# Attention scores on the two halves of TensorE's array, and one ring of eight banks

## The chip, the core and the metric

The kernel runs on one core of a Trainium2 chip. Its time is device microseconds; lower is better. TensorE (PE in the profile) multiplies and writes to PSUM, which has eight banks of 512 float elements a partition. VectorE (DVE) and ScalarE (ACT) read the banks, GpSimd (POOL) works in SBUF alone, SyncE (SP) issues the transfers.

## What is computed

Four layers over x, 4 sequences of 256 rows of 512 (8 tiles of 128 rows). Each layer normalises x, computes a gate from it (an FFN of the layer's own kind, then silu), and attention, and adds gate times attention to x. The attention, cut to what matters here:

```
q = x_n Wq -> 32 heads of 16;  k, v = x_n Wk, x_n Wv -> 8 heads (layers 0, 2, 3) or 32 (layer 1)
q, k = rope(q), rope(k)                                  # not in layer 1
s = q k^T / 4;  s = where(key <= query, s, -large)       # no mask in layer 1
out = softmax(s) v ;  x += gate * (out Wo)
```

Results are float32. Products of float32 precision are made of parts: `fp32r` operands that hold a high and a low part of each number.

## The kernel before, in words

**Units and groups.** Attention works on 8 units a layer; unit u is half of the heads (16) of sequence u // 2. A unit has 4 groups g of 4 heads, numbered through as gi = 4u + g. `project` makes q, k and v of 128 rows (tau 0 or 1), in three products in the layers with shared keys.

**Stacks.** `stack_high` (ScalarE) and `stack_low` (GpSimd) lay each head's 16 numbers out as 64: high, low, high part, then a place for the row maximum and zeros (keys: high, high, low, then a one and zeros), so that one product over 64 rows gives the precise score. `turn_stacks` turns them with TensorE, 128 columns at a time: two query heads lie under each other on 128 partitions. For keys the stack has four places, (k, 0, 0, k): turned, it gives one operand with the head's keys in the upper half and zeros in the lower, and one the other way round. ScalarE copies the turned queries to `qT` (`take_stacks`), VectorE the keys to `kT` (`take_key_stacks`).

**Scores, twice.** `scores_rows` (key "S", lines 685 and 691) makes scores with queries on the partitions, for two heads in one product of 2 x 128 or 2 x 256 columns because of the zeros, and adds the causal mask by another product (identity times mask). `row_max` (VectorE, L1370) takes the maximum. It runs LEAD = 5 groups ahead. `turn_max`, `take_max` and two transfers put the maxima into `qT` as the row that meets the one. `scores_cols` (key "ST", L719) makes the scores again with keys on the partitions, less the maximum; `exponentials` (ScalarE, L1038) empties them into `probs`; `cut_future` (GpSimd, L1572) clears the future. `weigh_values` (key "PV", L739) multiplies by the values: four heads in four column quarters of the array. `take_pv` (ScalarE) copies that out, `turn_context` (L750) turns it, `context` (VectorE, L1394, L1397) divides it. After every second unit `turn_rows` and `project_out` (L760, L780) finish a sequence, and `residual` adds it.

**Banks.** `Banks.claim` counts the uses of each bank, and TensorE waits until the earlier user is emptied. Row scores rotate over banks 0 and 1, column scores over 2 and 3, everything else (`misc_bank`) over 4 to 7. Each score bank holds one pair of heads and is emptied by itself.

**Order.** Every engine works through an order written out by hand, in `attention`. On TensorE one group is: `project` (g = 0: u+2, tau 1; g = 3: u+3, tau 0), `turn_max` (g = 3), column scores 0, stacks of one tau (g = 0: u+1, half 1; g = 2: u+2, half 0), row scores 0 of gi+5, values of gi-1, column scores 1, the stacks of the other tau, row scores 1, context of gi-2. In the last unit the next layer's normalised rows are turned too, through banks 0 and 1. The FFNs lie between the attentions.

## Time and profile before

| | |
|---|---|
| median of 3 runs | 1435.74 us (1433.23 to 1436.2) |
| profiled execution | span 1432.5 us, mean granted clock 0.970 |
| TensorE busy | 1328.4 us (93%) |
| VectorE, ScalarE, GpSimd busy | 884.6, 670.5, 389.4 us |

The span runs from the first to the last instruction; the median is 3.2 us above it. Matmuls are pipelined, so one lasts longer than the distance to the next start; distances between starts add up to time, durations don't. A row's "idle before" names what the engine waited for.

### The profile page before, as it was taken

What the parts mean: (1) busy time and instruction counts of PE and PEld (TensorE: products, weight loads), DVE (VectorE), ACT (ScalarE), POOL (GpSimd) and SP (SyncE); (2) the same over time, 40 slices, a digit from 0 to 9 for tenths busy, and PEclk for the clock granted to TensorE, in tenths of its full rate; (3) what the DMA queues carried; (4) which work ended last, traced back from release to release, by engine and by line L of the source; (5) the groups of instructions that cost most, each with busy time, mean ns of one, the idle gap of its engine ahead of it and who ended that gap; (6) DMA issues with size and microseconds to landing.
All of it is one profiled execution on the core that took longest, in us unless ns stands there. A gap on an engine that the chain in (4) does not pass through costs nothing.

```text
span 1432.5 us, 22066 instructions
## 1 busy us (share of the span) xinstructions
PE 1328.4 (93%) x8364; PEld 998.8 (70%) x8364; DVE 884.6 (62%) x1661; ACT 670.5 (47%) x1420; POOL 389.4 (27%) x470
## 2 busy tenths in 40 slices
PE   4999899997798999998899999989999879899997
PEld 3888777775465666665688888877777557677775
DVE  7733577777506655567455566467777645777873
ACT  3433365655133654556223333236565447365653
POOL 1000333323011100000433443323343346333331
PEclk9999999999799999999899999999999889999998
DMA  6000000002000000002222232100000300000001
GB/s 261 1 1 0 1 3 2 2 2 97 30 0 1 2 1 2 2 2 92 95 89 88 92 107 89 45 1 2 2 3 2 128 30 1 1 2 2 3 1 60
DMA packets 11610, 48.18 MB, mean 34 GB/s; under 512 B 2793, under 2 KB 3694, under 8 KB 10226
## 3 DMA queue, kind: packets, MB, share of 16 engines
q1 hardware_dynamic: 11506, 46.76, 9.3%
q8 instruction: 69, 1.13, 0.3%
q14 instruction: 35, 0.29, 0.1%
HBM read 44.13 MB, written 2.10 MB: 32 GB/s over the span
## 4 chain that ended last, share of the span: by engine, by line
PE 84%; DVE 10%; ACT 3%; issue 2%; DMA 1%; POOL 0%; SPq 0%; DVEq 0%; ACTq 0%
PE bank L487 18%; PE bank L647 13%; PE bank L518 9%; PE bank L719 7%; PE bank L780 7%; PE bank L685 7%; PE bank L739 7%; PE bank L665 6%; PE bank L691 3%; DVE negmaxs L1370 2%; PE bank L750 2%; DVE negmaxw L1370 2%; PE bank L588 1%; DVE stats L1127 1%; PE bank L760 1%
## 5 line engine op out<-in xcount | busy, mean ns | idle before, releaser
L1572 POOL TENSOR_SCALAR_AFFINE_SELECT probss<-probss 128x512 f32<-128x512 f32 x192 | 134.2, 700 | 334.0 <-ACT probss L1038 334.0
L1370 DVE TENSOR_REDUCE negmaxs<-bank 128x2 f32<-128x512 f32 (+1 forms) x384 | 193.7, 551 | 36.8 <-PE bank L691 35.0
L1038 ACT ACTIVATE probss<-bank 128x256 f32<-128x256 f32 (+1 forms) x384 | 167.9, 492 | 41.9 <-PE bank L719 41.4
L685 PE MATMUL bank<-kTs,qTs 128*128 128x512 f32 (+1 forms) x384 | 135.3, 411 | 5.2 <-DVE kTs L1378 2.8
L1518 POOL TENSOR_TENSOR W_lo<-W_lo_whole,W_hi 128x1536 fp32r<-128x1536 f32 x28 | 98.1, 3504 | 138.4 <-ACT W_hi L889 138.4
L719 PE MATMUL bank<-qTs,kTs 128*128 128x256 f32 (+1 forms) x384 | 117.3, 383 | 4.6 <-ACT probss L1038 3.9
L691 PE MATMUL bank<-mask,identb 128*128 128x256 bf16 x384 | 105.0, 283 | 0.0
L889 ACT ACTIVATE W_hi<-W_lo_whole 128x1536 fp32r<-128x1536 f32 x28 | 41.7, 1488 | 134.7 <-DVE W_lo_whole L1253 134.7
L1378 DVE CAST kTs<-bank 128x512 fp32r<-128x512 f32 x96 | 65.6, 689 | 50.9 <-PE bank L665 50.9
L1274 DVE TENSOR_TENSOR h_lo<-h_lo_whole,h_hi 128x512 fp32r<-128x512 f32 x50 | 73.3, 1465 | 34.9 <-ACT h_hi L911 34.9
L1378 DVE CAST kTw<-bank 128x512 fp32r<-128x512 f32 x64 | 40.9, 685 | 82.3 <-PE bank L665 82.3
L1370 DVE TENSOR_REDUCE negmaxw<-bank 128x2 f32<-128x512 f32 x128 | 81.6, 685 | 14.0 <-PE bank L685 13.6
L487 PE MATMUL bank<-xT_hi,W_hi 128*128 128x512 f32 x224 | 89.2, 398 | 0.0
L487 PE MATMUL bank<-xT_lo,W_hi 128*128 128x512 f32 x224 | 88.6, 396 | 0.0
L685 PEld LDWEIGHTS bank<-kTs,qTs 128*128 128x128 f32 x384 | 74.5, 194 | 20.0 <-DVE negmaxs L1370 11.5
L487 PE MATMUL bank<-xT_hi,W_lo 128*128 128x512 f32 x224 | 88.4, 395 | 0.0
L647 PE MATMUL bank<-Wqkv,xT_whole 128*128 128x512 f32 (+1 forms) x256 | 87.0, 495 | 0.8 <-ACT gate L922 0.8
L987 ACT ACTIVATE qks<-bank 128x320 f32<-128x320 f32 x48 | 21.1, 439 | 141.7 <-PE bank L647 141.6
L739 PE MATMUL bank<-probss,Vs 128*32 128x256 f32 (+1 forms) x1536 | 82.7, 333 | 4.0 <-issue 3.5
L911 ACT ACTIVATE h_hi<-h_lo_whole 128x512 fp32r<-128x512 f32 x72 | 45.4, 630 | 72.3 <-DVE h_lo_whole L1265 46.4
L1038 ACT ACTIVATE probsw<-bank 128x512 f32<-128x512 f32 x128 | 69.6, 599 | 16.6 <-PE bank L719 14.2
L719 PEld LDWEIGHTS bank<-qTs,kTs 128*128 128x128 f32 x384 | 60.4, 191 | 23.4 <-issue 12.7
(219 smaller groups left out, 3162.2 us busy)
## 6 DMA issues: line engine op xcount, KB each, us to landing
W_lo_whole<-in_w SPq DMA_DIRECT2D x28, 768.0 KB, 4.2
Wqkv_whole<-in_Wqkv SPq DMA_DIRECT2D x3, 1536.0 KB, 10.6
Wo_lo_whole<-in_Wo SPq DMA_DIRECT2D x4, 1024.0 KB, 6.2
Wqkv<-in_Wqkv SPq DMA_DIRECT2D x1, 3072.0 KB, 10.6
Wdown_whole<-in_Wd SPq DMA_DIRECT2D x1, 2816.0 KB, 15.2
x<-in_x SPq DMA_DIRECT2D x4, 512.0 KB, 5.9
out<-x SPq DMA_DIRECT2D x8, 256.0 KB, 2.2
V_lo_whole<-in_V SPq DMA_DIRECT2D x1, 1408.0 KB
```

Of the source, the lines that this page charges most:

```text
L487: ins = mm(ps[:], lh, rh, start=(c == 0), stop=(c == len(terms) - 1))
L518: ins = mm(B.tensor(key)[:], lh, rh, start=(j == 0 and c == 0), stop=(j == C - 1 and c == len(terms) - 1))
L647: ins = mm(ps[:, 0:width], lh, rh, start=(c == 0), stop=(c == len(terms) - 1))
L685: ins = mm(ps[:, 0:2 * nk].rearrange("p (h k) -> p h k", h=2), A[l].qT[u % 2][:, 2 * g + pl, qb * P:(qb + 1) * P], A[l].kT[u % 2][:, slot: ...
L691: ins = mm(dst, identb[:], mask[:].rearrange("p (h k) -> p h k", h=2), start=False, stop=True)
L719: ins = mm(ps[:, pairs[0] * nq:pairs[1] * nq].rearrange("p (h q) -> p h q", h=n), A[l].kT[u % 2][:, key_slot(l, g, 2 * g + pairs[0], par), ...
L739: ins = mm(ps[32 * i:32 * i + 32, q0:SEQ], A[l].Vflat[u % 4][:, (kb * A[l].vh + kv) * CELL:(kb * A[l].vh + kv) * CELL + 32], A[l].probs[gi ...
L780: ins = mm(ps[:], lh, rh, start=(c == 0), stop=(c == len(terms) - 1))
L1038: nc.scalar.activation(A[l].probs[gi % 2][:, kb, par:4:2, q0:SEQ], B.tensor(key)[:, 0:2 * nq].rearrange("p (h q) -> p h q", h=2), ACT.Exp, ...
L1370: v.tensor_reduce(A[l].negmax[u % 2][:, qb, 2 * g + pl:2 * g + pl + 9:8], B.tensor(key)[:, 0:2 * nk].rearrange("p (h k) -> p h k", h=2), A ...
L1378: v.tensor_copy(A[l].kT[u % 2][:, 4 * w:4 * w + 4, tau * P:(tau + 1) * P], B.tensor(key)[:].rearrange("p (a t) -> p a t", a=4)).then_inc(B ...
L1572: gp.affine_select(out=blk, in_=blk, compare_op=ALU.is_ge, fill=0.0, base=0, pattern=[[0, 4], [1, P]], channel_multiplier=-1).then_inc(cau ...
```

## The change

Score products use 64 rows: the heads of a pair lie in the two halves of the array, each product with its own half of `qT` and `kT`, and the two write to two neighbouring banks. The key stacks have no zero places and, where keys are shared, none twice, so a unit's turned keys are a fourth (shared) or half (layer 1) as wide. The heads are permuted on the host so that the two heads of a pair use different keys. The causal mask becomes products of 64 rows too: two for each half, each over 64 key columns of both heads.

A piece of scores, "S" or "ST" of one group and one block, now fills two banks and is emptied by one instruction of VectorE or ScalarE. All eight banks belong to one ring: pieces take banks 0-1, 2-3, 4-5, 6-7 in each group, then the ring is set to bank 0 and the values, the context and whatever follows take the next banks; `claim` waits for every earlier holder of the banks that it takes. TensorE's order within a group becomes: stacks of both taus at once (g = 0, 2), `project` and `turn_max`, then rows 0, columns 0, rows 1, columns 1, then values, context and the rest. ScalarE does both exponentials, then `stack_high`, then `take_pv`.

```diff
-    def claim(self, key, bank):
-        self.where[key] = (bank, self.uses[bank])
+    def claim(self, key, bank, n=1):
+        earlier = [self.emptied(k) for k in dict.fromkeys(self.holder[bank:bank + n]) if k is not None]
+        self.where[key] = (bank, self.uses[bank], n)
         self.uses[bank] += 1
+        self.holder[bank:bank + n] = [key] * n
+        return self.tensor(key), earlier
...
-            def misc_bank():
-                misc[0] += 1
-                return 4 + misc[0] % 4
+            def next_bank(n=1):
+                if n == 2:
+                    ring[0] += ring[0] % 2
+                bank = ring[0] % 8
+                ring[0] += n
+                return bank
...
-            def turn_stacks(l, u, tau, half):
+            def turn_stacks(l, u, half):
+                for tau in range(2):
+                    i = 2 * u + tau
                     pe.wait_ge(*pads.at(l, PADS[l]))
                     pe.wait_ge(*stack_hi.at(l, HI * (i + 1)))
                     pe.wait_ge(*stack_lo.at(l, 2 * (i + 1)))
+                    key = ("qT", l, u, tau, half)
+                    ps = claim(key, next_bank())
...
+                n = A[l].kn // 2
+                key = ("kT", l, u, half)
+                if GQA[l]:
+                    ps = claim(key, next_bank())[:, 0:2 * P].rearrange("p (t q) -> p t q", t=2)
+                else:
+                    ps = claim(key, next_bank(2), 2)
+                for tau in range(2):
+                    for p in range(n):
+                        ins = nc.tensor.transpose(ps[:, tau, p * P:(p + 1) * P].bitcast(F32R),
+                                                  A[l].kstack[tau][:, n * half + p, :, :].rearrange("p h s -> p (h s)"),
+                                                  ident_r[:])
...
+                key = ("S", l, u, g, qb)
+                ps = claim(key, bank, 2)
                 for pl in range(2):
...
-                    ins = mm(ps[:, 0:2 * nk].rearrange("p (h k) -> p h k", h=2),
-                             A[l].qT[u % 2][:, 2 * g + pl, qb * P:(qb + 1) * P],
-                             A[l].kT[u % 2][:, slot:slot + 2, 0:nk], start=True, stop=not CAUSAL[l])
+                    for par in range(2):
+                        r = slice(64 * par, 64 * par + 64)
+                        ins = mm(ps[:, par, pl * nk:(pl + 1) * nk], A[l].qT[u % 2][r, 2 * g + pl, qb * P:(qb + 1) * P],
+                                 A[l].kT[u % 2][r, key_slot(l, g, pl), 0:nk], start=(pl == 0),
+                                 stop=(pl == 1 and not CAUSAL[l]))
+                if CAUSAL[l]:
+                    for j in range(2):
+                        for par in range(2):
+                            r = slice(64 * par, 64 * par + 64)
+                            k0 = nk - P + 64 * j
+                            dst = ps[:, par, 0:2 * nk].rearrange("p (h k) -> p h k", h=2)[:, :, k0:k0 + 64]
+                            ins = mm(dst, cut_rows[r, j, :], cut_keys[r, j, :, :], start=False, stop=(j == 1))
+                ins.then_inc(B.fills(key), 1)
...
+                key = ("ST", l, u, g, kb)
+                ps = claim(key, bank, 2)
+                for pairs in ((0, 2),) if GQA[l] else ((0, 1), (1, 2)):
+                    n = pairs[1] - pairs[0]
+                    for par in range(2):
+                        r = slice(64 * par, 64 * par + 64)
+                        ins = mm(ps[:, par, pairs[0] * nq:pairs[1] * nq].rearrange("p (h q) -> p h q", h=n),
+                                 A[l].kT[u % 2][r, key_slot(l, g, pairs[0]), kb * P:(kb + 1) * P],
+                                 A[l].qT[u % 2][r, 2 * g + pairs[0]:2 * g + pairs[1], q0:SEQ], start=True, stop=True)
...
+                    if g == 0 and u + 1 < UNITS:
+                        turn_stacks(l, u + 1, 1)
+                    if g == 2 and u + 2 < UNITS:
+                        turn_stacks(l, u + 2, 0)
...
+                    for part in range(2):
+                        if ahead:
+                            scores_rows(l, gi + LEAD, part, 4 * part)
+                        scores_cols(l, u, g, part, 4 * part + 2)
+                    ring[0] = 0
                     if gi >= 1:
                         weigh_values(l, gi - 1)
                     if gi >= 2:
                         turn_context(l, gi - 2)
...
-                        transposes(l + 1, (2 * g - 2, 2 * g - 1), banks=(0, 1))
+                        transposes(l + 1, (2 * g - 2, 2 * g - 1))
...
                     exponentials(l, u, g, 0)
-                    if g == 0 and u + 1 < UNITS:
-                        take_stacks(l, u + 1, 0, 1)
-                    if g == 2 and u + 2 < UNITS:
-                        take_stacks(l, u + 2, 0, 0)
+                    exponentials(l, u, g, 1)
+                    if g < 2 and u + 2 < UNITS:
+                        stack_high(l, u + 2, g)
                     if gi >= 1:
                         take_pv(l, gi - 1)
...
+                key = ("S", l, u, g, qb)
+                dve.wait_ge(*B.filled(key))
+                v.tensor_reduce(A[l].negmax[u % 2][:, qb, :].rearrange("p (b h) -> p b h", b=2)[:, :, 2 * g:2 * g + 2],
+                                B.tensor(key)[:, :, 0:2 * nk].rearrange("p b (h k) -> p b h k", h=2),
+                                AX.X, ALU.max, negate=True).then_inc(B.empties(key), 1)
```

VectorE keeps its order: `row_max` of the first block, `rope` (g = 0 and 3), `row_max` of the second block, `context`.

## Rows read from the trace of the kernel before

**Rows 1.** The page: the chain that ended last, by engine

```profile
PE 84%; DVE 10%; ACT 3%; issue 2%; DMA 1%; POOL 0%; SPq 0%; DVEq 0%; ACTq 0%
```

**Rows 2.** Stretches (us; busy us of each engine, instructions; granted clock)

```profile
204.29:224.27 19.98, 19.94 (x179) 15.49 (x179) 15.50 (x38) 12.97 (x34) 7.83 (x13) 1.00 0.01 2
224.27:250.75 26.48, 26.44 (x212) 20.86 (x211) 19.97 (x46) 14.07 (x36) 8.78 (x13) 1.00 0.01 2
501.39:566.37 64.98, 64.61 (x429) 42.77 (x429) 37.04 (x71) 33.02 (x70) 5.72 (x8) 1.00 0.01 2
338.00:362.00 24.00, 12.93 (x122) 7.78 (x114) 20.92 (x60) 13.48 (x32) 8.46 (x11) 0.95 0.21 89
```

**Rows 3.** Timeline of TensorE, layer 0, 211.3 to 215: start, us, instruction

```profile
211.32 0.86 PE L739 MATMUL bank<-probss,Vs 128*32 128x256 f32 x16
212.11 0.38 PE L685 MATMUL bank<-kTs,qTs 128*128 128x256 f32 x1
...
212.62 0.48 PE L719 MATMUL bank<-qTs,kTs 128*128 128x256 f32 x2
213.14 0.49 PE L685 MATMUL bank<-kTs,qTs 128*128 128x512 f32 x1
...
213.95 0.38 PE L750 MATMUL bank<-ident,pvs 128*128 128x128 f32 x2
214.09 0.70 PE L719 MATMUL bank<-qTs,kTs 128*128 128x512 f32 x2
214.63 0.46 PE L665 MATMUL bank<-ident_r,qstacks 128*128 128x128 f32 x4
214.93 0.25 PE L665 MATMUL bank<-ident_r,kstacks 128*128 128x128 f32 x1
```

**Rows 4.** The chain in time, layers 0 and 1: one `project` each

```profile
218.85 2.12 PE bank L647 x12
...
472.74 5.19 PE bank L647 x16
```

**Rows 5.** Groups of VectorE, 204.29 to 250.75: busy us, mean ns, idle before

```profile
L1370 DVE TENSOR_REDUCE negmaxs<-bank 128x2 f32<-128x512 f32 x18 | 11.6, 684 | 0.8 <-PE bank L691 0.8
L1370 DVE TENSOR_REDUCE negmaxs<-bank 128x2 f32<-128x256 f32 x16 | 6.0, 419 | 0.8 <-PE bank L691 0.6
L1378 DVE CAST kTs<-bank 128x512 fp32r<-128x512 f32 x8 | 5.5, 689 | 4.9 <-PE bank L665 4.9
L1397 DVE TENSOR_TENSOR ctxs<-bank,recips 128x128 f32<-128x128 f32 x9 | 2.6, 291 | 0.3
...
L1394 DVE RECIPROCAL recips<-bank 128x8 f32<-128x8 f32 x9 | 1.8, 198 | 0.0
```

**Rows 6.** Timeline of VectorE: the first and last of rope's four products

```profile
208.81 0.48 DVE L1354 TENSOR_TENSOR rope_coss<-qks,cos 128x320 f32<-128x320 f32 x1
...
209.79 0.49 DVE L1361 TENSOR_TENSOR rope_coss<-rope_coss,rope_sins 128x320 f32<-128x320 f32 x1
```

**Rows 7.** Groups of ScalarE, 204.29 to 250.75

```profile
L1038 ACT ACTIVATE probss<-bank 128x512 f32<-128x512 f32 x16 | 8.7, 602 | 0.0
L1038 ACT ACTIVATE probss<-bank 128x256 f32<-128x256 f32 x16 | 5.3, 381 | 0.9 <-PE bank L719 0.7 <-issue 0.2
...
L1045 ACT ACTIVATE pvs<-bank 128x256 f32<-128x256 f32 x8 | 3.1, 388 | 2.9 <-PE bank L739 2.9
L1015 ACT ACTIVATE qstacks<-rope_coss 128x512 fp32r<-128x512 f32 x4 | 2.6, 638 | 0.0
L1021 ACT ACTIVATE kstacks<-rope_coss 128x128 fp32r<-128x128 f32 x8 | 2.1, 315 | 0.0
```

**Rows 8.** Groups of GpSimd, 204.29 to 250.75

```profile
L1556 POOL TENSOR_TENSOR qstacks<-rope_coss,qstacks 128x256 fp32r<-128x256 f32 x4 | 2.9, 734 | 2.0 <-ACT kstacks L1021 2.0
L1563 POOL TENSOR_TENSOR kstacks<-rope_coss,kstacks 128x128 fp32r<-128x128 f32 x4 | 1.9, 463 | 0.0
```

**Rows 9.** Timeline of TensorE at the start of layer 0's attention

```profile
167.80 0.75 PE L665 MATMUL bank<-ident_r,kstacks 128*128 128x128 f32 x4 [4.87 <-DVE kTs L1378]
```

More of the change, by code:

```diff
@@ L446, in transposes @@
                     key = ("xT", l, t)
-                    ps, again = B.claim(key, misc_bank() if banks is None else banks[t % 2])
-                    if again:
-                        pe.wait_ge(*B.before(key))
+                    ps = claim(key, next_bank() if banks is None else banks[t % len(banks)])
                     pe.wait_ge(*xn_ready.at(l, t + 1))
@@ L470, in gate_up @@
                     key = (("gate", "up")[which], l, n, j)
-                    ps, again = B.claim(key, 2 * (e % 2) + which)
-                    if again:
-                        pe.wait_ge(*B.before(key))
+                    ps = claim(key, 2 * (e % 2) + which)
                     terms = []
@@ L525, in out_tile @@
                 key = ("out", l, t)
-                ps, again = B.claim(key, bank)
-                pe.wait_ge(*B.before(key))
+                ps = claim(key, bank)
                 for c, (lh, rh) in enumerate(terms):
@@ L534, in weight_sum @@
                 key = ("wsum", m)
-                ps, again = B.claim(key, (0, 1, 4)[m])
-                if again:
-                    pe.wait_ge(*B.before(key))
+                ps = claim(key, (0, 1, 4)[m])
                 pe.wait_ge(*abs_summed.at(0, m + 1))
@@ L542, in low_rank_in @@
                 key = ("low", n)
-                ps, again = B.claim(key, n)
-                pe.wait_ge(*B.before(key))
+                ps = claim(key, n)
                 pe.wait_ge(*B.emptied(("xT", 3, 4 * n + 3)))
@@ L568, in ffn @@
                             key = ("group", c, which)
[L569 to L570 removed]
+                            ps = claim(key, (2 * c + which) % 4)
                             mm(ps[:], onehot[:, c * P:(c + 1) * P], src[:], start=True, stop=True).then_inc(B.fills(key), 1)
                         if c == 1:
[L573 removed]
+                            transposes(l, LATE_TILES, banks=(6, 7))
                     for t0 in (0, 4):
@@ L634, in project @@
                                        [(("qkv", l, u, tau), 0, 512), (("v", l, u, tau), 512, 256)]):
-                    ps, again = B.claim(key, misc_bank() if bank is None else bank)
-                    pe.wait_ge(*B.before(key))
+                    ps = claim(key, next_bank() if bank is None else bank)
                     terms = []
@@ L726, in weigh_values @@
                 key = ("PV", l, gi)
-                ps, again = B.claim(key, misc_bank())
-                pe.wait_ge(*B.before(key))
+                ps = claim(key, next_bank())
                 if CAUSAL[l]:
@@ L745, in turn_context @@
                 key = ("ctx", l, gi)
-                ps, again = B.claim(key, misc_bank())
-                pe.wait_ge(*B.before(key))
+                ps = claim(key, next_bank())
                 pe.wait_ge(*B.emptied(("PV", l, gi)))
@@ L755, in turn_rows @@
                     key = ("ctxT", l, b, tau)
-                    ps, again = B.claim(key, misc_bank())
-                    pe.wait_ge(*B.before(key))
+                    ps = claim(key, next_bank())
                     pe.wait_ge(*B.emptied(("ctx", l, 8 * b + 7)))
@@ L767, in project_out @@
                     key = ("O", l, b, tau)
-                    ps, again = B.claim(key, misc_bank())
-                    pe.wait_ge(*B.before(key))
+                    ps = claim(key, next_bank())
                     pe.wait_ge(*B.emptied(("ctxT", l, b, tau)))
@@ L788, in attention @@
                 for half in range(2):
-                    for tau in range(2):
-                        turn_stacks(l, 0, tau, half)
+                    turn_stacks(l, 0, half)
                 project(l, 2, 0)
```

314 lines of the change are left out of this document (129 added, 185 removed).

## The prediction

> **What bounds the kernel now.** The chain that ended last comes first: TensorE is on it for 84% of the span [rows 1]. The busy times by stretch say where: in layer 0's attention a unit of odd number takes 19.98 us with TensorE busy for 19.94, a unit of even number (it also turns and projects the context of a sequence) 26.48 us with 26.44, and two units of layer 1 take 64.98 us with 64.61 [rows 2]. The same rows say how near the others are: in the odd unit VectorE 15.50, ScalarE 12.97, GpSimd 7.83. So in a steady unit nothing but TensorE's work sets the time, because today no copy out of a bank is waited for: scores have banks 0 to 3, everything else turns through banks 4 to 7. The change takes work off TensorE and also takes that separation away. I therefore read both: the instructions removed, and then one unit step by step with the new waits. All my times are of the profiled execution, span 1432.5 us; the median of the runs, 1435.7, is 3.2 above it, and I add that at the end.
>
> **TensorE's score work.** One causal group today, by the starts in the timeline [rows 3]: row scores of the first query block (call them R0) from 212.11 to 212.62, 0.51 us; of the second block (R1) 213.14 to 213.95, 0.81; column scores of all queries (C0) 214.09 to 214.63, 0.54; of the late ones (C1) 212.62 to 213.14, 0.52. In sum 2.38 us. Around them: values (PV) 0.79, turning the context 0.14, four stack transposes 0.30, that is 0.075 us each.
> After the change every score matmul works on 64 rows and streams half the columns, with twice as many masks of half the width. Nothing in this trace splits the array by rows. Bounds: projection matmuls stream 384 columns in 2.12/12 = 0.177 us, 0.46 ns a column [rows 4]. Below, both halves stream at once and weights load for nothing: R0 0.24, R1 0.35, C0 0.24, C1 0.12, in sum 0.95. Above, nothing overlaps, and where matmuls are short each costs what a transpose with 128 new weight columns costs, 0.075: R0 8 x 0.075 = 0.60, R1 0.71, C0 0.47, C1 0.24, in sum 2.02. The nearest row is PV, whose matmuls use quarters of the array by columns: its 16 entries take 0.79 us, while plain fp32 entries of the whole array take 5.19/6144 columns = 0.84 ns a column [rows 4], so eight of 256 columns and eight of 128 would be 2.6 us. Quarters do run side by side, 3.3 times as fast. I take overlap for the streams but one weight load after another at 0.075: R0 0.55 (eight loads, bf16 ones a little cheaper), R1 0.60, C0 0.28, C1 0.18, in sum 1.61, 0.77 less than now.
> Of 32 stack transposes per causal unit 12 go (the zero slots and the doubled keys): 0.9 us; in layer 1 16 of 48: 1.2. Alone, this is 4 x 0.77 + 0.9 = 4.0 us off TensorE in a unit of 19.98.
>
> **What the others pay.** One reduce over two banks replaces two. The rows give 684 ns for 512 elements and 419 for 256 [rows 5], so 1.035 ns an element: 1024 elements 1.21 us (M1), and 512 elements 0.68 (M0). For the exponentials 602 and 381 [rows 7]: 1.04 us (E0) and 0.60 (E1). Only fixed parts go. The key copy falls from four of 689 ns to two of 256 elements, near 0.42 each; a second key copy on ScalarE, 0.31, goes from each stack [rows 5, 7]. These are real savings, but on engines that have slack.
>
> **What is late next: the banks.** After a group's four score pieces the ring is set to bank 0. So PV takes bank 0 and the context bank 1, both just held by R0; the next group's R0 takes banks 0 and 1 again, and `claim` waits until ScalarE has copied PV out and VectorE has finished `context`. In VectorE's order `context` stands behind both reduces and, for g = 0 and 3, behind `rope` between them: from 208.81 to 210.28 (the end of its last product), 1.47 us [rows 6]. In ScalarE's order the PV copy (0.39) stands behind both exponentials and, for g = 0 and 1, behind `stack_high` (0.64 and 0.31, which overlap a little: 0.80 for the two, an estimate) [rows 7]. And `turn_stacks` for u+2 now needs both halves at once, the second of which GpSimd ends only 1.20 us (0.73 + 0.46 [rows 8]) after `stack_high` in g = 1. Before, these were behind TensorE's back.
> I walk an odd causal unit from R0 to R0, with 0.27 us from the last matmul's start to the first use (the pair of context transposes lasts 0.38 against 0.14 to the next start [rows 3], so 0.24 and a little) and 0.06 where a wait ends. Group 1 to group 2: R0 0.55, C0 0.28, 0.25, E0 1.04, E1 0.58, stack_high 0.80, GpSimd 1.20, second query transposes 0.32, keys 0.16, waits 0.06: 5.24. Group 2 to 3: the query copy and C0's wait for it 0.75, C0 0.28, R1 0.60, 0.27, M1 1.21, 0.06, turn_max 0.14, project 2.11: 5.42. Group 3 to 0: R0 0.55, 0.27, M0 0.68, rope 1.47, M1 1.21, 0.06 (the keys' bank was R1's), keys 0.16, project 2.11: 6.51. Group 0 to 1: R0 0.55, 0.27, 0.68, 1.47, 1.21, context 0.20 + 0.29 [rows 5] with gaps 0.52, 0.06: 4.76. Sum 21.93 against 19.98: **+1.95**, although TensorE now has work for only 16 us of it.
> In an even unit the turning and projecting of the context, 26.48 - 19.98 = 6.5 us of TensorE, fills the waits of groups 2 and 3. Group 1 to 2 stays 5.24; group 2 to 3 ends with the turned rows (0.8 of the 6.5) in place of a wait, 5.81; group 3 to 0 is TensorE's own work, R0 to context 2.55 with two small waits, 5.7 of projecting, 0.7 of stacks, 2.11: 11.06; group 0 to 1 stays 4.76. Sum 26.87, **+0.39**.
> Layer 1 the same way, with M and E 1.21 and 1.04 throughout, no rope, R0 and R1 0.40, C0 and C1 0.32, `project` 5.19, key copies of 1.21 before R1: 30.0 for an odd unit and 38.4 for an even one against 64.98 for the pair: +1.4 and +2.0 by the split at the project pieces.
>
> **Starts and ends of the layers.** At a layer's start TensorE stands 4.87 us because four banks are not enough while VectorE does rope [rows 9]; with eight in the ring, and row scores that need only half 0's keys, the first reduce comes about 5 us sooner. I give each causal layer -5, layer 1 -6 (its 16 key copies become four larger ones). In the last unit (24.00 us, VectorE busy 20.92 [rows 2]) the next layer's transposes now take banks 2 and 3, which the next C0 needs: 0.8 us twice, +1.6 in three layers. Units 5 and 6, with less projecting and rope, come out 1.1 shorter together.
>
> **The sum.** Causal layers: 3 x 1.95 + 2 x 0.39 = +6.6, -1.1, -5, +1.6: +2.1, twice, and +0.5 for the last layer. Layer 1: 3 x 1.4 + 2 x 2.0 = +8.2, about -1.0 in units 5 and 6, -6, +1.6: +2.8. Total +7.5: span 1440, time **1443.5 us**. With the matmul bounds in the same walk: below, an odd unit is 1.57 shorter and an even one 1.67 (22 us over the three causal layers, 5 more in layer 1): 1416. Above, 0.7 and 1.06 longer: 1463.
>
> The Trainium skill bears on two steps. TensorEngine Tiling (Array Packing), section PSUM Bottleneck, says that tiling speeds TensorE up but not the emptying of PSUM, which may then be the limit; the trace agrees so far as VectorE has 15.5 us of work in 20. TensorE: Matmul & The Clock Gate, Part 3, says that matmuls in different row groups run concurrently; by it alone the sum would go to the lower bound, 1416. The Tiling page's Key Properties also say that a change of tiling mode drains the array, which speaks for the upper bound; no row separates such a drain.
>
> **The rivals.** (a) Slightly faster, by one mechanism: the two halves load and stream wholly at once, so the R and C pieces on the chain shrink to the lower bound. 1416, and everything between there and 1433. For it: PV's 3.3. It decides once R0 is under about 0.40 and R1 under 0.45.
> (b) The change does what it says and TensorE stays the bound: the new bank waits end before TensorE gets there. Then 4.0 us go from each causal unit (7 x 4.0 x 3 = 84), about 5 from each of layer 1's (35), and 20 at the starts: near 1300. Against it: the chain through VectorE in group 0 alone is 4.76 us, where TensorE has some 2.5 us of work.
> (c) The halves don't overlap: 1463 and somewhat more.
> (d) TensorE, idle for a quarter of each unit, is granted 1.2 instead of 2.4 GHz in the steady units: projections, PV and scores double, some 8 us a unit: 1600 and more. Against it: the last unit of layer 0 has TensorE busy for 12.93 of 24.00 us and a mean grant of 0.95 [rows 2].
> The change of the masks and the permuted heads cost nothing: host layout, and two casts more or less in layer 0's FFN behind a busy TensorE.
>
> **How the numbers follow.** My forecast, the waits eat the gain (1436 to 1455): 0.42. (a) 0.25, (b) 0.11, (c) 0.17, (d) 0.05. Within 0.2%, 2.9 us, which is about what a measurement of this kernel can tell from none, lies the seam between (a) and the forecast: 0.12, of which 0.10 is from the forecast and 0.02 from (a). Faster 0.34, slower 0.54. The likeliest case's own range is 1430 to 1460; for 8 in 10 I leave out (b)'s far end and (d): 1385 to 1480.
>
> **What would show it.** TensorE's busy share in a steady odd unit falls to about 0.75 to 0.8, with gaps before R0 ended by VectorE's `context` or ScalarE's PV copy, of 1 to 2 us in groups 0 and 1; an odd causal unit lasts 21 to 23 us; the row scores' group of eight starts about 70 ns apart; the start stall of 4.87 us shrinks. Wrong would be: gaps absent and units of 16 to 18 us (b), or starts 35 ns apart (a) or 120 ns apart (c).

## The result and the profile after

The changed kernel takes 1486.39 us (median of 4 runs, 1482.7 to 1487.8) against 1435.97 for the kernel before (1433.2 to 1440.7): ratio 1.0348, 95% interval 1.0324 to 1.0373, slower by 3.5%. The forecast, 1443.5 with a range of 1385 to 1480, had the sign and not the size; the measured time lies above the range. The profiled execution took 1486.46 us with a span of 1484.7, 52.2 more than before.

From the page of the changed kernel: the engines' shares of the chain that ended last, and the rows by slice of TensorE's busy time and granted clock.

```profile
PE   4999888887796888887799999988888679888887
...
PEclk7999889987697899999899999999898889999889
...
PE 70%; DVE 15%; ACT 6%; issue 5%; POOL 3%; DMA 1%; DVEq 0%; ACTq 0%; SPq 0%
```

TensorE's share of the chain fell from 84% [rows 1] to 70%; VectorE, ScalarE, GpSimd and "issue" took it over. The stretches that answer to [rows 2], in the same columns (length; busy TensorE, weight load, VectorE, ScalarE, GpSimd; granted clock), are two odd causal units (layer 2), an even one, and the same two units of layer 1 as before:

```profile
1002.24:1025.64 23.40, 19.38 (x198) 14.89 (x197) 13.16 (x26) 11.94 (x24) 7.31 (x13) 0.88 0.01 2
1025.64:1046.87 21.23, 17.84 (x200) 13.54 (x198) 13.37 (x28) 11.72 (x25) 7.18 (x12) 0.97 0.01 2
1046.87:1075.88 29.01, 25.85 (x232) 20.51 (x230) 17.91 (x34) 13.74 (x27) 7.34 (x12) 0.86 0.01 2
580.79:652.49 71.70, 60.13 (x428) 37.44 (x428) 30.95 (x43) 31.95 (x52) 5.66 (x8) 0.93 0.01 1
```

(The first of them is unit 0; the second, unit 1, is the plain odd unit.) TensorE's work in the odd unit is 17.84 us instead of 19.94, but the unit is longer. The clock column has something that [rows 2] hadn't: 0.97, 0.88, 0.86 and 0.93 in steady units, where before it was 1.00. One steady stretch cut at the changes of the grant, layer 2:

```profile
1013.00:1023.48 10.48, 8.19 (x92) 6.36 (x94) 7.79 (x17) 5.93 (x12) 3.72 (x6) 1.00 0.01 2
1023.48:1026.89 3.41, 3.41 (x36) 2.45 (x36) 1.92 (x2) 2.07 (x4) 0.97 (x2) 0.50 0.00 0
1026.89:1047.37 20.48, 17.09 (x202) 13.27 (x198) 12.85 (x27) 10.97 (x23) 6.21 (x11) 1.00 0.01 2
1047.37:1054.20 6.83, 5.83 (x56) 4.30 (x52) 3.33 (x6) 4.38 (x9) 2.81 (x6) 0.50 0.00 1
```

The grant drops to 0.50, that is to 1.2 GHz, for 3.41 and 6.83 us at a time. What goes before the second drop is to be seen in TensorE's timeline (start, us; in brackets idle time and what ended it), the counterpart of [rows 3]:

```profile
1043.11 0.44 PE L747 MATMUL bank<-ident,pvs 128*128 128x128 f32 x2
1045.52 0.44 PE L686 MATMUL bank<-kTs,qTs 64*128 64x128 f32 x4 [1.97 <-DVE ctxs L1374]
1045.78 0.31 PE L695 MATMUL bank<-cut_keys,cut_rows 64*128 64x128 bf16 x4
1045.88 0.50 PE L718 MATMUL bank<-qTs,kTs 64*128 64x512 f32 x2
1046.19 0.42 PE L686 MATMUL bank<-kTs,qTs 64*128 64x256 f32 x4
1046.43 0.31 PE L695 MATMUL bank<-cut_keys,cut_rows 64*128 64x128 bf16 x4
1046.52 0.39 PE L718 MATMUL bank<-qTs,kTs 64*128 64x256 f32 x2
1046.87 1.07 PE L737 MATMUL bank<-probss,Vs 128*32 128x256 f32 x16
...
1048.22 0.82 PE L655 MATMUL bank<-ident_r,qstacks 128*128 128x128 f32 x4
1050.04 0.72 PE L655 MATMUL bank<-ident_r,qstacks 128*128 128x128 f32 x4 [1.00 <-POOL kstacks L1530]
```

and in VectorE's over the same time:

```profile
1041.39 0.69 DVE L1343 TENSOR_REDUCE negmaxs<-bank 128x4 f32<-128x512 f32 x1 [2.25 <-PE bank L695]
1042.00 0.48 DVE L1329 TENSOR_TENSOR rope_coss<-qks,cos 128x320 f32<-128x320 f32 x1
...
1042.99 0.82 DVE L1336 TENSOR_TENSOR rope_coss<-rope_coss,rope_sins 128x320 f32<-128x320 f32 x1
1043.72 1.21 DVE L1343 TENSOR_REDUCE negmaxs<-bank 128x4 f32<-128x1024 f32 x1
1044.86 0.19 DVE L1371 RECIPROCAL recips<-bank 128x8 f32<-128x8 f32 x1
1045.08 0.29 DVE L1374 TENSOR_TENSOR ctxs<-bank,recips 128x128 f32<-128x128 f32 x1
```

R0 of group 1 stands 1.97 us, because its bank holds the context of group 0 and VectorE makes first maximum, rope, second maximum and context in that order, 3.98 us from 1041.39 to 1045.37. One group later the second query transposes stand 1.00 us for GpSimd's low rows, and the clock has dropped in between, at 1047.37: the matmuls after it start further apart (PV, which it catches halfway, lasts 1.07 instead of 0.86).

Whole layers, from the first start of PV(0) to that of PV(31), two rows of each timeline; in brackets what the prediction's terms add up to:

| | before | changed | difference | predicted |
|---|---|---|---|---|
| layer 0 | 162.14 | 180.34 | +18.2 | +7.1 |
| layer 1 | 211.67 | 234.47 | +22.8 | +8.8 |
| layer 2 | 160.69 | 178.89 | +18.2 | +7.1 |
| layer 3 | 156.72 | 167.93 | +11.2 | +5.5 |
| all else (starts, ends, FFNs) | | | -18.2 | -21 |

The starts did nearly what they should; the steady units did not, nor the last unit.

### The profile page after: what moved, and what is told of

The parts are those of the page before. It is cut to its first block, busy times and chain, and to the rows that moved or that the text cites. A ratio compares the mean times of both kernels' runs of the same rounds, so it can differ in the third digit from the quotient of the medians.

```text
span 1484.7 us, 22636 instructions
## 1 busy us (share of the span) xinstructions
PE 1271.3 (86%) x8844; PEld 951.8 (64%) x8844; DVE 809.6 (55%) x1309; ACT 643.4 (43%) x1100; POOL 368.6 (25%) x462
## 4 chain that ended last, share of the span: by engine, by line
PE 70%; DVE 15%; ACT 6%; issue 5%; POOL 3%; DMA 1%; DVEq 0%; ACTq 0%; SPq 0%
PE bank L490 17%; PE bank L642 12%; PE bank L520 9%; PE bank L775 7%; PE bank L737 5%; PE bank L686 4%; DVE negmaxs L1343 4%; PE bank L718 3%; PE bank L747 2%; PE bank L655 2%; DVE negmaxw L1343 2%; PE bank L667 1%; POOL probss L1539 1%; PE bank L584 1%; PE bank L695 1%
## 5 line engine op out<-in xcount | busy, mean ns | idle before, releaser
L1343 DVE TENSOR_REDUCE negmaxs<-bank 128x4 f32<-128x512 f32 x192 | 180.8, 955 | 106.9 <-PE bank L695 105.0
L1019 ACT ACTIVATE probss<-bank 128x1024 f32<-128x1024 f32 x192 | 146.8, 809 | 116.3 <-PE bank L718 115.8
L686 PE MATMUL bank<-kTs,qTs 64*128 64x128 f32 (+1 forms) x768 | 93.9, 323 | 47.2 <-DVE ctxs L1374 35.9
L686 PEld LDWEIGHTS bank<-kTs,qTs 64*128 64x128 f32 x768 | 75.9, 210 | 73.4 <-issue 45.7
L1343 DVE TENSOR_REDUCE negmaxw<-bank 128x4 f32<-128x1024 f32 x64 | 74.9, 1218 | 67.5 <-PE bank L686 67.5
L718 PE MATMUL bank<-qTs,kTs 64*128 64x256 f32 (+1 forms) x384 | 92.4, 470 | 20.4 <-DVE xT_lo L1127 7.5
L1008 ACT ACTIVATE qTs<-bank 128x512 fp32r<-128x512 f32 x96 | 54.0, 600 | 86.6 <-PE bank L655 85.3
L1019 ACT ACTIVATE probsw<-bank 128x1024 f32<-128x1024 f32 x64 | 62.8, 1023 | 38.8 <-PE bank L718 38.7
L642 PE MATMUL bank<-Wqkv_hi,xT_hi 128*128 128x384 f32 x192 | 69.7, 363 | 0.0
L655 PE MATMUL bank<-ident_r,qstacks 128*128 128x128 f32 x384 | 49.8, 273 | 22.7 <-POOL kstacks L1530 15.5
## 6 DMA issues: line engine op xcount, KB each, us to landing
Wqkv<-in_Wqkv SPq DMA_DIRECT2D x1, 3072.0 KB, 11.2
```

Of the source, the lines that this page charges most:

```text
L642: ins = mm(ps[:, 0:width], lh, rh, start=(c == 0), stop=(c == len(terms) - 1))
L655: ins = nc.tensor.transpose(ps[:, p * P:(p + 1) * P].bitcast(F32R), A[l].qstack[tau][:, 8 * half + 2 * p:8 * half + 2 * p + 2, :] .rearran ...
L686: ins = mm(ps[:, par, pl * nk:(pl + 1) * nk], A[l].qT[u % 2][r, 2 * g + pl, qb * P:(qb + 1) * P], A[l].kT[u % 2][r, key_slot(l, g, pl), 0: ...
L718: ins = mm(ps[:, par, pairs[0] * nq:pairs[1] * nq].rearrange("p (h q) -> p h q", h=n), A[l].kT[u % 2][r, key_slot(l, g, pairs[0]), kb * P: ...
L1019: nc.scalar.activation(A[l].probs[gi % 2][:, kb, :, q0:SEQ].rearrange("p (b h) q -> p b h q", b=2), B.tensor(key)[:, :, 0:2 * nq].rearrang ...
L1343: v.tensor_reduce(A[l].negmax[u % 2][:, qb, :].rearrange("p (b h) -> p b h", b=2)[:, :, 2 * g:2 * g + 2], B.tensor(key)[:, :, 0:2 * nk].re ...
```

## The experiments

All edits are of the changed kernel (1486.4 us). Ratios are to the kernel before. The share of the span at 1.2 GHz is worked out as 2 x (1 - mean clock), since there are only two levels: for the changed kernel (0.908) 18.4% or 273 us, before (0.970) 86 us.

**1. Orders: `e1_pv_copy_first`, `e2_rope_last`.** Theory 1: waits for the common banks, and the clock that falls with them, set the time. Theory 2: the 64-row matmuls themselves cost.

```diff
                     exponentials(l, u, g, 1)
+                    if gi >= 1:
+                        take_pv(l, gi - 1)          # e1
                     if g < 2 and u + 2 < UNITS:
                         stack_high(l, u + 2, g)
-                    if gi >= 1:
-                        take_pv(l, gi - 1)
```
```diff
-                    rope(l, ...)                    # e2: g = 0 and 3
                     if ahead:
                         row_max(l, gi + LEAD, 1)
                     if gi >= 2:
                         context(l, gi - 2)
+                    rope(l, ...)
```

> The changed kernel, except that ScalarE copies the weighted values out of their bank before it stacks the high rows (0.8 us in groups 0 and 1), not after. Changed kernel: 1486.4 us. Theory 1 (TensorE waits for banks of the common ring, and the idle time also brings the 1.2 GHz grants): in groups 0 and 1 the row scores may start up to 0.8 us earlier, but the stacks come later by 0.4 and most waits of the trace end with VectorE's context, so 3 to 15 us less, 1471 to 1483. Theory 2 (the matmuls of 64 rows cost TensorE more than the ones of 128 did, waits are not the matter): no change, 1483 to 1490.

> The changed kernel, except that VectorE's rope products of groups 0 and 3 (1.47 us) stand behind the second maximum and the context instead of between the two maxima. Theory 1: the row scores and the context's bank come free 1.47 us earlier in two groups of four, 2 x 21 units x up to 1.5 us = up to 60 us; the rope parts come later, which takes some back: 1440 to 1470. Theory 2: no change, 1483 to 1490.

Measured: 1519.2 (1.0584, 1.0560 to 1.0607), 33 us slower than the changed kernel, and 1458.0 (1.0167, 1.0148 to 1.0186), 28 us faster. Rope last fits theory 1. The copy's move went the other way than I said. The transposes of the query stacks, as the page groups them, say why; first the changed kernel, then e1 (busy, mean ns, then idle before and what ended most of it):

```profile
L655 PE MATMUL bank<-ident_r,qstacks 128*128 128x128 f32 x384 | 49.8, 273 | 22.7 <-POOL kstacks L1530 15.5
```

```profile
L655 PE MATMUL bank<-ident_r,qstacks 128*128 128x128 f32 x384 | 52.3, 283 | 35.1 <-POOL kstacks L1530 28.6
```

The waits for GpSimd's rows nearly double, from 15.5 to 28.6 us, while R0's 35.9 us for the context stay. What I counted as a slack of 0.4 us on the stacks was on the path, and the clock went down too (0.890, 334 us at 1.2 GHz). Theory 2 is out as the whole cause: the same matmuls in another order differ by 61 us.

**2. The old separation of banks: `e3_split_rings`, `e4_split_and_order`.**

```diff
-                bank = ring[0] % 8
+                bank = 4 + ring[0] % 4
...
-                            scores_rows(l, gi + LEAD, part, 4 * part)
-                        scores_cols(l, u, g, part, 4 * part + 2)
-                    ring[0] = 0
+                            scores_rows(l, gi + LEAD, part, 0)
+                        scores_cols(l, u, g, part, 2)
```

This is e3; the row pieces ahead of a layer's first group and the next layer's transposes go to banks 0 and 1 with it. e4 adds TensorE's and ScalarE's old order.

> The changed kernel's instructions in the changed order, but row scores always in banks 0 and 1, column scores in banks 2 and 3, all else turns through banks 4 to 7, as before the change. The waits for context and for the copy of the weighted values go. In their place the second row scores wait in the same group for the first maximum (0.68 or 1.21 us after the first row scores, with only 0.28 us of column scores between). Theory 1: a different set of waits of about the same length, 1450 to 1490. Theory 2: no change, 1483 to 1490. By itself this run tells little; it is the step to the next one.

> As the run with split banks, and TensorE's order is that of the kernel before: first column scores, first row scores, weighted values, second column scores, second row scores; ScalarE copies the weighted values between its two exponentials. All matmuls of 64 rows, the merged copies out of two banks and the smaller stacks stay. Theory 1: each wait has 0.8 us or more of TensorE work beside it, an odd causal unit takes 17.5 to 19.5 us instead of 21.2 to 23.4, the 1.2 GHz stretches become few: 1375 to 1430, faster than the changed kernel by 4% or more. Theory 2: the matmuls cost what they cost, 1470 or more.

Measured: 1566.9 (1.0925, 1.0887 to 1.0963) and 1559.2 (1.0864, 1.0816 to 1.0911). My 1375 to 1430 for e4 was a bad miss, and e3 lies far above its 1450 to 1490. Both were granted only 0.89. Rows of e4's timeline with idle time, one odd unit and a little:

```profile
1079.28 0.44 PE L642 MATMUL bank<-Wqkv_hi,xT_hi 128*128 128x384 f32 x1 [1.85 <-DVE ctxs L1375]
...
1087.98 0.44 PE L686 MATMUL bank<-kTs,qTs 64*128 64x128 f32 x4 [1.78 <-DVE negmaxs L1344]
...
1092.44 0.51 PE L655 MATMUL bank<-ident_r,qstacks 128*128 128x128 f32 x4 [1.76 <-POOL kstacks L1531]
```

Its odd units have three waits of 1.8 us in place of one of 2 and one of 1 to 1.6. One is the row scores': a piece now fills two banks, so two banks for row scores hold one piece and not two, and R0 waits for the maximum of the R1 ahead of it, a whole reduce of 1.2 us. Separate rings were free while each bank was emptied alone; emptying two at once takes the double buffering that they lived from. The other two, a projection behind the context and the stacks behind GpSimd, are not of this kind, and no run has separate rings with banks emptied singly, so how much of the 73 us above the changed kernel is the lost double buffering is not shown. The orders and rings of before alone don't give the time of before.

**3. Is the clock a cause? `e9_filler` and its control `e17_filler_elsewhere`.** If idle time brings the 1.2 GHz stretches, then useless work inside the waits must make the kernel faster.

```diff
+            def fill(ps, n):
+                for _ in range(n):
+                    nc.tensor.transpose(ps[:, 0:P].bitcast(F32R), ident_r[:], ident_r[:])
...
+                                fill(B.ps[:, 2, :], 16)    # e9: group 1, causal layers
                             scores_rows(l, gi + LEAD, part, 4 * part)
...
+                        fill(ps, 12)                       # e9: turn_stacks, half 0, tau 1
                     pe.wait_ge(*pads.at(l, PADS[l]))
...
+                            fill(B.ps[:, 2, :], 28)        # e17 instead: group 3, behind project
```

The first bank filled is one that the next column scores overwrite, and TensorE waits first until it is empty. In `turn_stacks` of e9 the claim of the bank moves ahead of the waits for the stacks, so that there is a bank to fill; nothing is issued in between. e9 adds 552 transposes in all, e17 504.

> The changed kernel with extra TensorE work that nobody reads: 16 transposes of the identity into the next column bank before the row scores of group 1 (where the trace has a wait of 1.97 us in each steady causal unit), and 12 before the second query transposes of group 2 (wait 0.3 to 1.6 us), in the three causal layers. Order, waits and all other work are unchanged; the extra transposes cost about 75 ns each where nothing is waited for. Theory A (the idle time of TensorE brings the stretches at 1.2 GHz, and these are a good part of the loss): the waits are filled, most 3.4 us stretches at 0.5 in steady causal units vanish, odd units settle at 21.2 us instead of 21.2 to 23.4: 1445 to 1475. Theory B (the lost time is the bank waits alone; the granted clock falls for another reason, such as the 64-row matmuls): the stretches stay, and time is equal or up to 25 us longer: 1484 to 1512.

> A control for the extra transposes: the changed kernel with the same kind of transposes, 28 together behind the projection of group 3, where TensorE waits for nothing, instead of 16 and 12 inside the two waits. Theory A (what helped was that TensorE was not idle in the waits): the waits of 2.0 and 1.6 us stay and the stretches at 0.5 with them, and the transposes cost 28 x 75 ns = 2.1 us and more in each of 18 units: 1515 to 1540. Theory B (more TensorE work anywhere raises the grant, or the other edit of that kernel helped): 1465 to 1500.

Measured: e9 1463.8 (1.0201, 1.0182 to 1.0220), 22.6 us **faster with more work**; e17 1533.6 (1.0688, 1.0668 to 1.0707), 47 us slower. Stretches of e9: units 1 and 2 of layer 2, and nearly all of its units 0 to 6 in one piece.

```profile
1014.94:1036.42 21.48, 19.63 (x227) 15.83 (x226) 13.48 (x28) 11.85 (x25) 7.18 (x12) 1.00 0.01 2
1036.42:1063.47 27.05, 25.57 (x261) 21.02 (x259) 17.77 (x34) 13.06 (x27) 7.36 (x12) 1.00 0.01 2
995.63:1149.23 153.60, 139.51 (x1530) 110.88 (x1529) 97.67 (x192) 79.38 (x154) 45.86 (x77) 1.00 0.08 32
```

The same stretch of layer 2 in the changed kernel, and in e17:

```profile
996.17:1139.53 143.36, 122.83 (x1204) 93.93 (x1203) 86.12 (x163) 74.54 (x144) 43.41 (x72) 0.88 0.01 2
```

```profile
1001.00:1158.00 157.00, 134.02 (x1280) 107.33 (x1284) 86.24 (x163) 70.08 (x138) 39.66 (x65) 0.87 0.01 2
```

153.6 us without one drop, against means of 0.88 and 0.87. The waits are still there in e9, only shorter for TensorE (rows with the filler L647):

```profile
1011.37 1.57 PE L647 MATMUL bank<-ident_r 128*128 128x128 f32 x16
1013.59 0.44 PE L692 MATMUL bank<-kTs,qTs 64*128 64x128 f32 x4 [0.65 <-DVE ctxs L1384]
...
1016.29 1.20 PE L647 MATMUL bank<-ident_r 128*128 128x128 f32 x12
1018.00 0.51 PE L661 MATMUL bank<-ident_r,qstacks 128*128 128x128 f32 x4 [0.51 <-POOL kstacks L1540]
```

In e17 R0's wait stays whole:

```profile
1064.79 0.44 PE L690 MATMUL bank<-kTs,qTs 64*128 64x128 f32 x4 [1.97 <-DVE ctxs L1382]
```

Units 1 to 6 of the three causal layers had a mean grant of 0.90, 0.90 and 0.88 in the changed kernel, 0.94, 0.91 and 0.94 in e17, and 1.00 in all three in e9. So more work elsewhere took some of the drops away and left most in layer 2; about the same work inside the waits took all. The control is not wholly clean: its fill itself stands 0.73 us for a bank, and a wait of 1.00 us for a maximum is new behind it. Theory A holds in these units: TensorE's idle time in the bank waits is what brings 1.2 GHz, at least most of it. In e9 12.6% of the span, 184 us, are left at that level, at the ends and starts of layers and in layer 1, where no filler was put. 89 us less at half speed gave 24 us of span (44 would be the most, had all of it been TensorE's work, and the transposes that outlast a wait cost something). The four stretches from PV(0) to PV(31) are 30 us shorter, all else 6 us longer, for which no run gives a reason.

**4. Which waits can be ordered away: `e10_cols_first`, `e11_cols_first_rope_last`, `e12_cols_rope_late`, `e14_ring2`.** e10 has columns before rows within a part. e11 is e10 with rope last. e12 is e11 with the first half of the next stacks turned and copied in group 3 instead of 2. e14 is the changed kernel with `ring[0] = 2` in place of `ring[0] = 0`.

> The changed kernel, except that in each group the column scores are issued ahead of the row scores of the same part (C0 R0 C1 R1 instead of R0 C0 R1 C1), same banks. In group 1 R0 waits 1.97 us for VectorE's context while C0, whose banks are free, stands behind it, and with it ScalarE's exponential, its high rows of the stack, GpSimd's low rows and the transposes of group 2. Theory 1 (waits in a row behind the common banks set the unit): C0 and all that follows start up to 2 us earlier in group 1, an odd causal unit falls from 21.2 to 19.5 to 20.5 us: 1445 to 1475. Theory 2 (VectorE's own sequence of two maxima, rope and context is the loop that sets the unit): no gain, 1480 to 1495.

> The column scores first, and VectorE's rope products behind its second maximum and the context (alone this gave 1458.0). Theory 1: the two gains add in part, as they shorten different waits (row scores on context, stacks on GpSimd): 1420 to 1450. Theory 2: as the rope-last kernel alone, 1455 to 1465.

> The same with the first half of the next stacks turned in group 3 instead of group 2, so that GpSimd's low rows have a group more. In group 3 the transposes (0.6 us) stand ahead of the projection. Theory 1: the last wait for GpSimd's stacks goes, 5 to 20 us less than the kernel without this edit: 1410 to 1440. Against it: the stack copies crowd into group 3 and 0 on VectorE and ScalarE, whose maximum and rope stand there: 0 to 20 us more.

> The changed kernel with one number altered: after each group the common ring is set to bank 2 instead of bank 0. Weighted values and turned context then take the banks that the first column scores (C0) have left, the next row scores R0 find banks 0 and 1 free, and the next C0 is what waits for ScalarE's copy and VectorE's context. Theory 1 (R0 waiting for the context with VectorE's rope and both maxima in front is the main wait): R0 and so the first maximum start up to 2 us earlier in group 1, odd causal units 18.5 to 20.5 us, few stretches at 1.2 GHz: 1420 to 1465. Theory 2 (the wait only moves from R0 to C0, and C0 leads the stacks): 1480 to 1500.

Measured: e10 1507.4 (1.0506, 1.0487 to 1.0526), e11 1457.5 (1.0155, 1.0137 to 1.0173), e12 1446.6 (1.0076, 1.0057 to 1.0095), e14 1507.4 (1.0502, 1.0480 to 1.0523). In e10, the same place of the order as above:

```profile
1025.06 0.50 PE L718 MATMUL bank<-qTs,kTs 64*128 64x512 f32 x2
1028.24 0.54 PE L686 MATMUL bank<-kTs,qTs 64*128 64x128 f32 x4 [2.68 <-DVE ctxs L1374]
...
1044.61 0.37 PE L667 MATMUL bank<-ident_r,kstacks 128*128 128x128 f32 x2 [1.54 <-DVE negmaxs L1343]
```

The columns do start early, but R0, which feeds VectorE, now comes later, and the wait for the context grows from 1.97 to 2.68 us: VectorE's sequence is the loop, so theory 2 was right for this edit, and worse than it said. The odd unit has three more waits, 1.54 us for a maximum and twice about 0.75 for copies of ScalarE. The loss is waits and not clock: the mean grant was 0.920, above the changed kernel's 0.908. With rope out of the middle (e11) the edit costs and gives nothing beside e2's 1458.0, as theory 2 had it. Late stacks (e12) give 11 us more, within the 5 to 20 foreseen for them, but 1446.6 lies above the 1410 to 1440 of its theory 1. In e14 the wait moves and splits, as its theory 2 had it, and costs more than its 1480 to 1500:

```profile
1043.86 0.86 PE L737 MATMUL bank<-probss,Vs 128*32 128x256 f32 x16 [0.65 <-ACT probss L1019]
...
1046.58 0.50 PE L718 MATMUL bank<-qTs,kTs 64*128 64x512 f32 x2 [0.99 <-DVE ctxs L1374]
...
1048.25 0.86 PE L737 MATMUL bank<-probss,Vs 128*32 128x256 f32 x16 [0.64 <-ACT probss L1019]
...
1050.73 0.51 PE L655 MATMUL bank<-ident_r,qstacks 128*128 128x128 f32 x4 [0.96 <-POOL kstacks L1530]
```

Values wait 0.4 to 0.65 us in every group for the exponential that empties C0's banks; once a unit C0 waits 0.99 for the context and the stacks 0.96 for GpSimd.

**5. All waits together: `e15_ring2_rope_late`, `e18_pv0_rest2`, `e19_pv0_rest2_pv_first`, `e20_best`.** e15 is e14 with rope last and late stacks. e18 gives the values bank 0 again and lets only the rest go on from bank 2; e19 adds e1's edit; e20 adds the lines with a condition (`steady` is true while the groups of a layer run; e18 and e19 set `ring[0] = 2` behind the values without one):

```diff
-                    ring[0] = 0
+                    ring[0] = 2 if CAUSAL[l] and g == 1 else 0    # e20; e18, e19: 0
                     if gi >= 1:
                         weigh_values(l, gi - 1)
+                    if ring[0] == 1:
+                        ring[0] = 2
...
+                if steady[0] and ring[0] == 8:                    # e20, in next_bank
+                    ring[0] = 4
```

> The same with VectorE's rope behind the second maximum and the context, and the first half of the next stacks turned in group 3. Theory 1: what C0 waits for comes 1.47 us earlier in groups 3 and 0 and GpSimd's stacks are never waited for; odd causal units 17 to 19 us with TensorE's own work of 16 us in them: 1370 to 1425, under the kernel before. Theory 2: 1440 to 1465, as the best order so far (1446.6) had it.

> The changed kernel with three edits: after each group only the weighted values take bank 0, and the common ring goes on from bank 2; rope last on VectorE; the first half of the next stacks in group 3. Theory 1 (the changed kernel's matmuls are cheaper and only bank waits and the 1.2 GHz stretches they bring hide it): the wait of 0.64 us ahead of the weighted values in every group, which the kernel with the ring at bank 2 had, becomes at most 0.4 us ahead of the row scores in one or two groups of four; 1385 to 1425, below the kernel before. Theory 2 (VectorE's and ScalarE's chains set the groups at this length whatever the banks): 1432 to 1450, no faster than the kernel before.

> The same, and ScalarE copies the weighted values ahead of the high rows of the stack. Alone in the changed kernel this edit cost 33 us, since the stacks were what group 2 waited for. With the stacks a group later nothing waits for them, and row scores may start 0.8 us earlier in groups 1 and 2: 0 to 15 us below the run without it. If the stacks are still waited for: 5 to 20 us above it.

> The fastest kernel so far (1407.0 us) with two more edits of the banks: in group 1 of the causal layers the weighted values take bank 2 instead of bank 0, where they waited 1.42 us for VectorE's first maximum; and the common ring goes from bank 7 back to bank 4 instead of into banks 0 and 1, so that the row scores don't wait 0.64 us for a projection's copy in even units. Theory 1 (each such wait is paid in full, and again by 1.2 GHz stretches): 0.8 us in each of 18 units and 0.7 in each of 9, 15 to 25 us: 1380 to 1395. Theory 2 (the wait moves to the next column scores, which need the same copies): 1400 to 1412.

| | us | ratio to before (95%) | clock | share at 1.2 GHz |
|---|---|---|---|---|
| e15 | 1438.3 | 1.0018 (1.0005 to 1.0031) | 0.939 | 12.2% |
| e18 | 1420.2 | 0.9886 (0.9862 to 0.9910) | 0.931 | 13.8% |
| e19 | 1407.0 | 0.9799 (0.9784 to 0.9815) | 0.938 | 12.4% |
| e20 | 1387.0 | 0.9662 (0.9647 to 0.9677) | 0.947 | 10.6% |

e15 missed its 1370 to 1425 and ends just under the 1440 of its theory 2; e18, e19 and e20 came out within the ranges of their first theories. e19's edit, which alone cost 33 us, gives 13 once the stacks come a group later: it was the stacks, as expected. e20 is 3.4% faster than the kernel before and 99 us faster than the changed one, with the same matmuls and copies. Its odd and even causal units in layer 2, and the same two kinds, even first, in layer 0:

```profile
968.17:986.49 18.32, 16.47 (x198) 13.08 (x198) 13.73 (x29) 11.97 (x25) 7.16 (x12) 1.00 0.01 3
1030.59:1056.61 26.02, 23.54 (x230) 18.55 (x231) 17.68 (x34) 13.08 (x27) 7.17 (x12) 1.00 0.01 2
223.43:250.88 27.45, 24.98 (x232) 19.38 (x232) 17.67 (x34) 13.25 (x27) 7.17 (x12) 0.94 0.01 2
250.88:270.63 19.75, 17.95 (x200) 13.95 (x200) 13.68 (x28) 12.15 (x25) 7.15 (x12) 0.91 0.01 2
```

18.32 and 26.02 at clock 1.00, against 19.98 and 26.48 [rows 2]. Of the 18 units 1 to 6 of the causal layers only the two shown from layer 0 had a drop, one of 3.41 us each, and they took some 1.5 us longer than their like. The waits that are left in the shown kinds of units are each under 0.8 us, with and without a drop:

```profile
1010.34 0.44 PE L689 MATMUL bank<-kTs,qTs 64*128 64x128 f32 x4 [0.34 <-ACT pvs L1033]
...
1012.36 0.86 PE L740 MATMUL bank<-probss,Vs 128*32 128x256 f32 x16 [0.64 <-ACT probss L1026]
...
1014.83 0.50 PE L721 MATMUL bank<-qTs,kTs 64*128 64x512 f32 x2 [0.75 <-DVE ctxs L1381]
```

## Why the prediction was right about the sign and wrong about the size

**TensorE's savings: right in sum, not in their parts.** In the timeline above R0, C0, R1 take 0.36, 0.31 and 0.33 us by their starts, C1 0.35 to the values; sum 1.35 (1.54 in the group at 1058.08), predicted 1.61, before 2.38. But I had 0.55, 0.28, 0.60 and 0.18. The four R1 matmuls of 64x256 take 0.24 us from their first start to the first mask's, 60 ns each, half of the 118 that 256 columns need alone by [rows 4]: there the two halves streamed wholly side by side, and my "one weight load after another at 0.075" was wrong. The eight entries of R0 and of R1 start 45 and 41 ns apart, nearer to the 35 that I named for rival (a) than to my 70, and both pieces are under the 0.40 and 0.45 that I named as its mark. C1, on the other hand, was twice as long as said; why is not shown. So (a)'s mechanism came true for the row scores, and the kernel still became slower.

**The waits at full clock: the walk was nearly right for causal layers.** It gave 21.93 and 26.87 us for odd and even units. The changed kernel's plain odd unit takes 21.23 at 0.97, and e9, where the clock stays up, 21.48 and 27.05. The named places were right too: R0 on the context (predicted chain in group 0 4.76 us, measured 4.55 by the starts of PV) and the stacks on GpSimd. Layers 0 and 2 came to +8.8 and +9.6 in e9, whose units 1 to 6 have full clock (unit 0 and the last do not), against +7.1 predicted. Units 5 and 6, which I had 1.1 us shorter together, were 1.2 shorter in e9's layer 2. (Two sums of mine were slightly off: by its own figures the lower bound takes 24 us off the causal layers, not 22, and 1440 and 3.2 make 1443.2.)

**The step that failed is rival (d), the clock, priced as all or nothing at 0.05.** I took it that TensorE either keeps 2.4 GHz, because one stretch of the last unit with 12.93 us of work in 24.00 showed 0.95 [rows 2], or has 1.2 GHz through all steady units, 1600 us. The runs showed neither: single drops of 3.4 to 13.7 us beside waits of 1 to 2 us, mean 0.86 to 0.97 by unit. An even unit was granted 0.86 and took 29.01 us instead of 26.87, the unit 0 in the first row 23.40 at 0.88, and in unit 5 of each causal layer one drop of 13.65 us followed R0's wait of 2.16 us: 19.65 us in layer 2 against 16.20 in e9. The row that I held against the clock was also cut too early. It ends 2.16 us into a drop of the kernel before, inside a wait of 6.64 us that TensorE has at the end of the layer:

```profile
359.84:370.08 10.24, 7.05 (x20) 5.64 (x21) 3.59 (x10) 1.19 (x2) 0.00 (x0) 0.50 0.00 0
```

Up to there the grant had held at 1.00 with TensorE busy for 8.82 of 15.44 us (344.40 to 359.84). The row's 0.95 was therefore no sign that idle time is harmless; it mixed a stretch that kept the clock with the start of one that lost it. Across the span this is 273 us at half speed instead of 86, and at least 24 us of the 45 that the forecast was short (52.2 against 7.5), by e9. The two effects add: a wait is paid as idle time, and where the grant falls behind it, again as slower work. The other 21 us are not split by any run. TensorE: Matmul & The Clock Gate in the Trainium skill, section A second HAM failure mode: psum-queue depth-cycling, says of another kernel that short idles between groups of matmuls, from cycling through PSUM banks, make the clock swing between its levels; the trace agrees (drops of 3.41 and 6.83 us beside waits of 1.97 and 1.00), and I had not weighed it.

**Last units: a term mis-sized.** I gave them +1.6 us. From the start of PV(28) to PV(31) layer 2 took 12.22 before and 17.26 in the changed kernel. Its rows:

```profile
1167.02 1.94 PE L457 MATMUL bank<-ident,xn 128*128 128x128 f32 x8 [1.92 <-DVE xn L1140]
1170.71 1.01 PE L718 MATMUL bank<-qTs,kTs 64*128 64x512 f32 x4 [1.76 <-DVE xT_lo L1127]
```

The next layer's transposes wait 1.92 us for VectorE's normalised rows, as they did before (1.83), but now C0 then waits 1.76 more behind them until VectorE has emptied those banks, and 1.50 us in the next group, and 13.65 us of the 17.26 are at clock 0.50. I had put 0.8 us twice, at full clock. In layers 0 to 2 this is some 11 us above the forecast.

**Layer 1: the rest.** +22.8 against +8.8, with last unit included. Its even units took 40.8 to 40.9 us (predicted 38.4); in e9 one fell to 38.27 where no drop met it, though nothing there had been edited. The last unit is 3.6 of the 14 us above the forecast; how the others split between waits and clock was not tested.

**Starts of layers: right.** -18.2 us outside the PV(0) to PV(31) stretches against -21.

Of the rivals, (a) and (b) fell: R0 and R1 were as short as (a) asked, but TensorE's work was not what set the unit. The gain that they promised comes, in part, once banks are assigned otherwise: e20. (c) was nearest in time (1463) for a wrong reason. The Trainium skill, TensorEngine Tiling (Array Packing), section PSUM Bottleneck, told the direction: it says that tiling speeds up TensorE but not the emptying of PSUM, and here R0 waits 1.97 us until VectorE has emptied a bank.

## What to carry to other kernels

When work is taken off the engine that sets the time, walk one steady unit with every bank's earlier holder; then ask for each wait what the granted clock does after it: filling waits with useless work alone was worth 22.6 us here. Merging two banks into one piece halves the number of buffers: count buffers in pieces, not in banks. Choose which short-lived result takes which just-emptied bank by the order in which the emptying engines work; here three such choices, with two reordered engines and stacks a group later, took nearly 7% off.

## What was unexpected of the hardware

The grant fell in units in which TensorE was busy for 84 to 89% of the time (17.84 of 21.23, 25.85 of 29.01), with single idle stretches of up to 2.2 us and no longer. Filling 2.8 us of waits in a unit of 21.5 with transposes nobody reads brought it back to 1.00 for 153.6 us. In e20 waits of 0.3 to 0.85 us did not bring it down in 16 of 18 units (16.47 of 18.32 us busy in the one shown), but did in two of layer 0 with the same waits. Two halves of the array gave 60 ns a matmul of 256 columns instead of 118 in the row scores, while a whole group's scores still took 1.35 to 1.54 us, above the 0.95 of the bound.
